# A post-norm decoder layer on one core: transposing softmax rows in halves, a residual sum kept in PSUM, and another order of VectorE and GpSimd work

## Chip, core and metric

The kernel runs on one core of a Trainium2 chip. The metric is the device time of one execution, in microseconds (us). The engines are PE (TensorE; PEld is its weight load), DVE (VectorE), ACT (ScalarE), POOL (GpSimd) and SP (SyncE, which issues most DMAs).

## What is computed

For 16 sequences of 128 rows of width 128, all in fp32:

```python
x = layernorm(x + attention(x))          # 16 heads of 64, softmax over 128 keys
x = layernorm(x + cross_attention(x, c)) # softmax over the 16 heads, inside each row
x = layernorm(x + feed_forward(x))       # light branch 64 wide, heavy branch 512 wide
```

The top-k of the reference takes 128 rows of 128, so the heavy branch is computed for every row.

## The kernel before, in words

**Steps.** One sequence of the batch is one unit of work, and three of them are in flight. In step s (0 to 15, then a tail written out by hand) the first attention of sequence s is begun (a), the first attention of s-1 is ended and its cross attention begun (b, c), and the cross attention of s-2 is ended (d). Some projections are made for four sequences at once, so the steps differ by their phase, s modulo 4: phase 0 has the larger part of the first attention's queries and keys, phase 1 has the keys of the cross attention, phase 2 has neither, and phase 3 begins the queries of the next group (`project_qk(g + 1, "A")`). Steps 3 to 14 run in a loop of four steps, three times; the others are written out. Every engine has its own list of instructions, in the order in which the program names them, and the engines wait for each other through counting semaphores (`wait_ge`).

**PE in a step** goes through this list, which L1242 to L1375 write out: transposes of the second eight heads of the step before (L1243); projections, if the phase has any; `values` (L1156); `weighted` (L1148, softmax times values); `scores(0)` (L1223, heads 0 to 7); `project_o` (L1168); `transpose_p2` (L1055); `scores(1)`; `values2` (L1162 to L1164); the transpose of x1 (L1308) and of the normalised x2 (L1083); `weighted_v2` (L1067); `project_q2` (L1136); transposes of the first eight heads (L1345); in phase 3 the first projections of the next group (L1028 to L1030); `project_o2` (L1076); `scores2` (L1178); in phases 3 and 0 further projections.

**The transposes of the softmax** (`transpose_p`, L1120; the instruction is L1127). A call makes four transposes of 128x128, one per head, into one PSUM bank; two calls make eight heads. ACT copies each bank to `pt` (L534).

**From scores to transposes.** DVE takes the row maxima of four heads at a time (`score_max`, L807), ACT makes the exponentials and their sums (L541, eight heads are q = 0 and 1, or 2 and 3), DVE inverts the sums of eight heads (`inverse_sums`, L813), POOL multiplies eight heads by them (L414) and PE transposes them.

**From project_o to x1.** DVE adds the residual to the bank of `project_o` (L769, `t1` lies in SBUF), takes the statistics (L771, L775), POOL makes the root (L383, L385), and DVE normalises (`x1_out`, L779). Between L775 and `x1_out` DVE does the two halves of `block_diagonal` (L718), of which PE's `weighted_v2` needs both. POOL waits for x1, adds a bias to it (L389), and then does L414.

**Behind project_q2** DVE takes out its two banks (`q2_out`, L785), and between them half of the cross attention's output (`regrouped`, L699; ACT does the other half at L499). `project_o2` waits for both halves and for the first `q2_out`, `scores2` for the second. In phase 3 the first projection of the next group waits for the first `q2_out`, the second for the second, the fourth for DVE's `regrouped`.

**First steps.** The weights of queries and keys come in five parts (`QK_PARTS`, L282) and are split into a high and a low fp32r part by ACT (L459) and DVE (L666). In step 1 DVE also scales and splits the weights of the feed forward (L915 to L920).

## Time and profile before

| | |
|---|---|
| runs of the kernel (us) | 406.04, 406.34, 407.11; median 406.34 |
| the profiled execution | 407.05 us, its span 405.2 us, granted clock 0.998 of full speed |
| busy in the span (us) | PE 394.5, PEld 343.2, DVE 286.9, ACT 240.5, POOL 146.7 |
| POOL's multiplications of the softmax, L414 | 32, 60.7 us |
| PE's transposes of the softmax, L1127 | 256, 34.6 us |

A busy PE is counted from the start of a product to its modelled end, and a product's neighbours overlap it. So the pace of PE is read from the start of one block of products to the start of the next, and not from the mean duration.

### The profile page before, as it was taken

To read this page: it belongs to the slowest core of one execution; us is meant where nothing else is said; L and a number is where in the kernel's file an instruction comes from. 1 tells how busy PE (TensorE), PEld (TensorE's weight loads), DVE (VectorE), ACT (ScalarE), POOL (GpSimd) and SP (SyncE) were. 2 spreads that over 40 slices of the span, in tenths; PEclk is the share of its full clock that TensorE was granted. 3 is DMA by queue.
4 is the path that set the end of the run, shared out by engine and by line. 5 is a ranking of instruction groups with operands and counts; after the bars stand their busy time and mean duration, and the time that the engine had idled before them with its cause. 6 is when DMAs were issued, how large, how long until landed. Compare 5 with 4: busy or idle time off the path is not lost.

```text
span 405.2 us, 15945 instructions
## 1 busy us (share of the span) xinstructions
PE 394.5 (97%) x6580; PEld 343.2 (85%) x6580; DVE 286.9 (71%) x662; ACT 240.5 (59%) x814; POOL 146.7 (36%) x223
## 2 busy tenths in 40 slices
PE   8999999999999999999999999999999999999995
PEld 7797788788888888788888888888988888898985
DVE  4685786865758687866849678676848778687645
ACT  5685664745666584745567475645558566555552
POOL 0541444331523354331413454422415454323314
PEclk9999999999999999999999999999999999999999
DMA  7900112210110213110110213100101111211001
GB/s 244 371 27 8 43 25 63 65 37 2 33 31 11 46 29 91 37 28 8 32 25 15 49 29 92 34 21 8 42 15 24 41 39 23 47 39 26 27 28 52
DMA packets 43758, 19.33 MB, mean 48 GB/s; under 512 B 36592, under 2 KB 41200, under 8 KB 43696
## 3 DMA queue, kind: packets, MB, share of 16 engines
q1 hardware_dynamic: 42880, 16.88, 16.1%
q0 software_dynamic: 528, 1.45, 1.0%
q8 instruction: 52, 0.85, 0.8%
q10 hardware_dynamic: 288, 0.07, 0.1%
q14 instruction: 10, 0.08, 0.1%
HBM read 8.95 MB, written 1.05 MB: 25 GB/s over the span
## 4 chain that ended last, share of the span: by engine, by line
PE 85%; DVE 6%; SPq 3%; issue 2%; ACT 2%; DMA 1%; POOL 0%; POOLq 0%; DVEq 0%
PE ps L1223 7%; PE ps L1168 7%; PE ps L1048 7%; PE ps L1076 7%; PE ps L1148 7%; PE ps L1127 6%; PE ps L1136 6%; PE ps L1028 5%; PE ps L1030 4%; PE ps L1029 4%; PE ps L1178 4%; PE ps L1067 3%; SPq L317 3%; PE ps L1104 3%; PE ps L1162 2%; PE ps L1156 2%
## 5 line engine op out<-in xcount | busy, mean ns | idle before, releaser
L541 ACT ACTIVATE p<-ps,neg_max 128x128 f32<-128x128 f32 x256 | 90.3, 385 | 40.8 <-DVE neg_max L807 40.8
L414 POOL TENSOR_TENSOR p<-p,row_inv 128x1024 f32<-128x1024 f32 x32 | 60.7, 1898 | 60.2 <-DVE row_inv L813 60.2
L534 ACT ACTIVATE pt<-ps 128x512 f32<-128x512 f32 x62 | 34.3, 624 | 48.6 <-PE ps L1127 48.5
L541 ACT ACTIVATION_READ_ACCUMULATOR p<-ps,neg_max 128x1 f32 x256 | 57.9, 226 | 0.0
L807 DVE TENSOR_REDUCE neg_max<-ps 128x4 f32<-128x512 f32 x64 | 41.6, 673 | 4.8 <-PE ps L1223 4.0
L753 DVE TENSOR_TENSOR ot<-ps,bv 128x512 f32<-128x512 f32 x32 | 22.0, 689 | 27.6 <-PE ps L1148 27.5
L1136 PE MATMUL ps<-x1t,wq 128*64 128x64 f32 x1024 | 33.8, 224 | 1.6 <-DVE v2s L763 0.9
L1127 PE MATMUL ps<-ident,p 128*128 128x128 f32 x256 | 34.6, 279 | 0.8 <-POOL p L414 0.8
L1223 PE MATMUL ps<-kt,qt 64*64 64x128 f32 x1024 | 35.2, 275 | 0.0
L1136 PEld LDWEIGHTS ps<-x1t,wq 128*64 128x64 f32 x1024 | 31.5, 138 | 3.0 <-issue 1.9
L1168 PE MATMUL ps<-wo,ot 128*128 128x128 f32 x256 | 32.7, 281 | 0.6 <-DVE ot L753 0.6
L1168 PEld LDWEIGHTS ps<-wo,ot 128*128 128x128 f32 x256 | 29.9, 191 | 3.3 <-issue 3.2
L1148 PEld LDWEIGHTS ps<-pt,v 128*64 128x64 f32 x512 | 27.6, 137 | 5.8 <-issue 5.8
L1223 PEld LDWEIGHTS ps<-kt,qt 64*64 64x64 f32 x1024 | 27.6, 132 | 5.5 <-issue 5.3
L1076 PE MATMUL ps<-wo,ot 128*128 128x128 f32 x256 | 31.9, 278 | 0.0
L1076 PEld LDWEIGHTS ps<-wo,ot 128*128 128x128 f32 x256 | 30.0, 192 | 1.8 <-issue 0.2
L1148 PE MATMUL ps<-pt,v 128*64 128x128 f32 x512 | 31.5, 276 | 0.0
L1127 PEld LDWEIGHTS ps<-ident,p 128*128 128x128 f32 x256 | 27.6, 141 | 3.6 <-POOL p L414 0.9
L1048 PE MATMUL ps<-cg,wk 128*64 128x128 f32 x512 | 29.7, 274 | 0.0
L394 POOL TENSOR_TENSOR rn<-ssm,minus_half 128x1 f32<-128x1 f32 x16 | 8.8, 551 | 55.9 <-DVE ssm L744 55.9
L1048 PEld LDWEIGHTS ps<-cg,wk 128*64 128x64 f32 x512 | 27.8, 137 | 1.2 <-issue 1.0
L1028 PE MATMUL ps<-xg_hi,wqk_hi 128*128 128x512 f32 x63 | 26.2, 416 | 2.2 <-DVE qt L785 1.4
(152 smaller groups left out, 835.5 us busy)
## 6 DMA issues: line engine op xcount, KB each, us to landing
v<-v2s SPq DMA_DIRECT2D x256, 32.0 KB
xg<-x_t SPq DMA_DIRECT2D x4, 256.0 KB, 2.9
cg<-ctx_t SPq DMA_DIRECT2D x4, 256.0 KB, 3.4
wo<-w_o SPq DMA_DIRECT2D x2, 512.0 KB, 9.5
xres<-x_nat SPq DMA_DIRECT2D x15, 64.0 KB, 1.8
pt<-w_qk SPq DMA_DIRECT2D x3, 256.0 KB, 4.3
out<-x2b SPq DMA_DIRECT2D x3, 256.0 KB, 2.3
x2b<-w_v SPq DMA_DIRECT2D x1, 512.0 KB, 7.3
```

What stands on the lines that cost most here:

```text
L414: nc.gpsimd.tensor_tensor(ph, ph, row_inv[:, 8 * half:8 * half + 8].unsqueeze(2).to_broadcast([T, 8, T]), ALU.mult).then_inc(p_ready, 1)
L534: nc.scalar.activation(pt[:, u * BANK:(u + 1) * BANK], bank(T_BANK[u]), ACT.Copy).then_inc(pt_ready, 1)
L541: last = nc.scalar.activation(p[:, hd * T:(hd + 1) * T], bank(S_BANK[q])[:, pos * T:(pos + 1) * T], ACT.Exp, bias=neg_max[:, hd:hd + 1], a ...
L807: nc.vector.reduce_max(neg_max[:, first:first + 7:2], bank(S_BANK[q]).rearrange("p (h k) -> p h k", h=4), AX.X, negate=True).then_inc(max_ ...
L1028: nc.tensor.matmul(out_cols, w_hi_cols, m_hi, start=True, stop=False)
L1048: last = nc.tensor.matmul(bank(BLOCK_BANKS[blk][r])[64 * ih:64 * ih + 64, i * 128:(i + 1) * 128], wk2[:, hd * DH:(hd + 1) * DH], own, star ...
L1076: last = nc.tensor.matmul(bank(O2, D), ot2[:, k * 128:(k + 1) * 128], wo2[:, k * D:(k + 1) * D], start=k == 0, stop=k == K - 1)
L1127: last = nc.tensor.transpose(bank(T_BANK[u])[:, i * T:(i + 1) * T], p[:, hd * T:(hd + 1) * T], ident[:])
L1136: last = nc.tensor.matmul(bank(Q2[u])[64 * ih:64 * ih + 64, i * HALF:(i + 1) * HALF], wq2[:, hd * DH:(hd + 1) * DH], x1t[:, ih * HALF:(ih ...
L1148: last = nc.tensor.matmul(bank(PV_BANK[u])[64 * (i % 2):64 * (i % 2) + 64, (i // 2) * T:(i // 2 + 1) * T], v[b_par][:, hd * DH:(hd + 1) * ...
L1168: last = nc.tensor.matmul(bank(O, D), ot[:, c * T:(c + 1) * T], wo[:, c * D:(c + 1) * D], start=c == 0, stop=c == NC - 1)
L1223: mm = nc.tensor.matmul(bank(S_BANK[2 * half + i % 2])[qh * HALF:(qh + 1) * HALF, (i // 2) * T:(i // 2 + 1) * T], qt[rows, first:first + H ...
```

## The change

- `transpose_p` takes eight heads in a call. Each head is transposed in two halves of 64 rows: the half e reads rows 64e to 64e+63 of `p` and the matching corner of the identity and writes 64 columns. The two halves of a head go to two different banks, so that a bank ends with half the queries of eight heads and no longer with four whole heads; ACT's copies put the pieces where they belong (`pt_part`, runs of 64 elements). Both banks of eight heads are released together at the end.
- `t1` is now the bank of `project_o` itself: the sum is written back to PSUM, and the statistics and `x1_out` read it there. `weighted_v2`, which writes that bank, waits for x1 and no longer for the sum.
- POOL multiplies the first eight heads right behind the root and adds the bias to x1 after that.
- DVE inverts the first eight sums between the two halves of `block_diagonal`, ahead of `x1_out`. `regrouped` goes ahead of both `q2_out` in phases 0 to 2 and behind both in phase 3.
- Step 1 on DVE: `score_max(2)` ahead of `x1_out`, the second inversion between the two `q2_out`. The high part of the feed forward's weights is made by ACT in step 2, the low part by DVE at the end of step 2.
- The first part of the query weights has 256 columns and not 128, and the third projection's two products with the high weights go ahead of the wait for the low ones.

```diff
...
@@ -195,6 +194,14 @@
+        def pt_part(u):
+            half, e = u // 2, u % 2
+            return (pt[:, half * 8 * T:(half + 1) * 8 * T].rearrange("p (h e q) -> p e h q", h=8, e=2)[:, e],
+                    bank(T_BANK[u]).rearrange("p (h q) -> p h q", h=8))
+        t1 = bank(O, D)
         def ot2_half(k2):
@@ -279,7 +286,7 @@
-        QK_PARTS = [slice(0, 128), slice(128, BANK)] + [slice(u * BANK, (u + 1) * BANK) for u in range(1, 4)]
+        QK_PARTS = [slice(0, 256), slice(256, BANK)] + [slice(u * BANK, (u + 1) * BANK) for u in range(1, 4)]
         HALVES = [slice(0, BANK), slice(BANK, 2 * BANK)]
@@ -383,6 +390,8 @@
                 nc.gpsimd.tensor_tensor(rs1[:], ve1[:], minus_half[:, 0:1], ALU.pow).then_inc(rs1_ready, 1)
+            def x1_biased(s, b_par):
                 if isinstance(s, int) and s == 1:
@@ -393,6 +402,13 @@
                 nc.gpsimd.tensor_tensor(x2b[:, bass.ds((s - 2) * D, D)], x2[:], bdl_row[:], ALU.add).then_inc(x2b_ready, 1)
+            def over_sum(s, half):
+                pool.wait_ge(inv_ready, 2 * s + half + 1)
+                ph = p[:, half * 8 * T:(half + 1) * 8 * T].rearrange("q (h k) -> q h k", h=8)
+                nc.gpsimd.tensor_tensor(ph, ph, row_inv[:, 8 * half:8 * half + 8].unsqueeze(2).to_broadcast([T, 8, T]),
+                                        ALU.mult).then_inc(p_ready, 1)
@@ -406,13 +422,12 @@
                     rstd1(s, b_par)
-                for half in range(2):
-                    if a:
-                        pool.wait_ge(inv_ready, 2 * s + half + 1)
-                        ph = p[:, half * 8 * T:(half + 1) * 8 * T].rearrange("q (h k) -> q h k", h=8)
-                        nc.gpsimd.tensor_tensor(ph, ph, row_inv[:, 8 * half:8 * half + 8].unsqueeze(2).to_broadcast([T, 8, T]),
-                                                ALU.mult).then_inc(p_ready, 1)
+                if a:
+                    over_sum(s, 0)
+                if bc:
+                    x1_biased(s, b_par)
+                if a:
+                    over_sum(s, 1)
                 if d:
...
@@ -531,7 +547,8 @@
                     act.wait_ge(mm_t, 4 * s + u + 1 if u < 2 else 4 * s - 4 + u + 1)
-                    nc.scalar.activation(pt[:, u * BANK:(u + 1) * BANK], bank(T_BANK[u]), ACT.Copy).then_inc(pt_ready, 1)
+                    dst, src = pt_part(u)
+                    nc.scalar.activation(dst, src, ACT.Copy).then_inc(pt_ready, 1)
@@ -607,6 +624,9 @@
                     exponentials(3)
+                if static and s == 2:
+                    act.wait_ge(wup_scaled, 2)
+                    nc.scalar.activation(wup_hi[:], wup, ACT.Copy).then_inc(wup_split, 1)
                 if static and s == 0:
...
@@ -766,9 +787,9 @@
                 dve.wait_ge(xres_ready, s)
-                nc.vector.tensor_tensor(t1[:], bank(O, D), xres[b_par][:], ALU.add).then_inc(sum1_ready, 1)
+                nc.vector.tensor_tensor(t1, bank(O, D), xres[b_par][:], ALU.add).then_inc(sum1_ready, 1)
                 dve.wait_ge(sum1_ready, s)
-                nc.vector.bn_stats(st1[:], t1[:]).then_inc(stats1_ready, 1)
+                nc.vector.bn_stats(st1[:], t1).then_inc(stats1_ready, 1)
@@ -776,7 +797,7 @@
                 dve.wait_ge(rs1_ready, s)
-                nc.vector.tensor_scalar(x1[:], t1[:], mv1[:, 0:1], rs1[:, 0:1], ALU.subtract, ALU.mult).then_inc(x1_ready, 1)
+                nc.vector.tensor_scalar(x1[:], t1, mv1[:, 0:1], rs1[:, 0:1], ALU.subtract, ALU.mult).then_inc(x1_ready, 1)
@@ -852,7 +873,12 @@
                     block_diagonal(s, 0)
+                if a and bc:
+                    inverse_sums(0)
+                if d:
                     block_diagonal(s, 1)
+                if static and s == 1:
+                    score_max(2)
                 if bc:
@@ -871,8 +897,7 @@
                     return
-                if a:
-                    inverse_sums(0)
+                if a and not (static and s == 1):
                     score_max(2)
@@ -889,16 +914,19 @@
                         dve.wait_ge(in_own_j, 16)
+                    if d and phase < 3:
+                        regrouped(s)
                     q2_out(s, 0)
-                if d:
-                    regrouped(s)
-                if bc:
+                    if static and s == 1:
+                        inverse_sums(1)
                     q2_out(s, 1)
+                    if d and phase == 3:
+                        regrouped(s)
                 if phase == 0 and a and bc:
                     qk_out(g + 1, "A")
-                if a:
+                if a and not (static and s == 1):
                     inverse_sums(1)
@@ -914,8 +942,7 @@
                     nc.vector.tensor_scalar(wup[:, FH:FP], wup[:, FH:FP], gam[:, 0:1], D ** 0.5, ALU.mult, ALU.mult).then_inc(wup_scaled, 1)
-                    dve.wait_ge(wup_scaled, 2)
-                    nc.vector.tensor_copy(wup_hi[:], wup).then_inc(wup_split, 1)
+                if static and s == 2:
                     dve.wait_ge(wup_split, 1)
@@ -1117,15 +1144,18 @@
-            def transpose_p(n, u):
-                if u % 2 == 0:
-                    pe.wait_ge(p_ready, 2 * n + u // 2 + 1)
-                for i in range(4):
-                    hd = 4 * u + i
-                    last = nc.tensor.transpose(bank(T_BANK[u])[:, i * T:(i + 1) * T], p[:, hd * T:(hd + 1) * T], ident[:])
-                last.then_inc(mm_t, 1)
+            def transpose_p(n, half):
+                pe.wait_ge(p_ready, 2 * n + half + 1)
+                for i in range(8):
+                    hd = 8 * half + i
+                    for e in range(2):
+                        rows = slice(HALF * e, HALF * e + HALF)
+                        mm = nc.tensor.transpose(bank(T_BANK[2 * half + e])[:, i * HALF:(i + 1) * HALF],
+                                                 p[rows, hd * T:(hd + 1) * T], ident[rows, rows])
+                        if i == 7:
+                            mm.then_inc(mm_t, 1)
@@ -1234,14 +1264,18 @@
                     nc.tensor.matmul(bank(FIRST_BANKS[0]), wqk_hi[:, 0:128], xg_lo[:], start=False, stop=True).then_inc(mm_qk, 1)
+                    project_qk(0, "A", lambda r: None, FIRST_BANKS, units=(1,))
+                    pe.wait_ge(w_hi, 2)
+                    nc.tensor.matmul(bank(FIRST_BANKS[2]), wqk_hi[:, 256:384], xg_hi[:], start=True, stop=False)
+                    nc.tensor.matmul(bank(FIRST_BANKS[2]), wqk_hi[:, 256:384], xg_lo[:], start=False, stop=False)
                     pe.wait_ge(w_lo, WQK_SPLIT[0])
-                    project_qk(0, "A", lambda r: None, FIRST_BANKS, units=(1, 2, 3))
+                    nc.tensor.matmul(bank(FIRST_BANKS[2]), wqk_lo[:, 256:384], xg_hi[:], start=False, stop=True).then_inc(mm_qk, 1)
+                    project_qk(0, "A", lambda r: None, FIRST_BANKS, units=(3,))
                     pe.wait_ge(w_lo, WQK_SPLIT[1])
                 if bc:
-                    transpose_p(s - 1, 2)
-                    transpose_p(s - 1, 3)
+                    transpose_p(s - 1, 1)
                 if phase == 0 and a and bc:
@@ -1315,7 +1349,7 @@
                     if bc:
-                        pe.wait_ge(sum1_ready, s)
+                        pe.wait_ge(x1_ready, s)
                     weighted_v2(s, 0)
...
```

## Rows read from the trace of the kernel before

**Rows 1.** The profile page, busy time of the engines in the span.
```profile
PE 394.5 (97%) x6580; PEld 343.2 (85%) x6580; DVE 286.9 (71%) x662; ACT 240.5 (59%) x814; POOL 146.7 (36%) x223
```

**Rows 2.** Waits of PE: who waited for whom, us in total, times, longest.
```profile
PE ps L1028 <- DVE qt L785: 1.4, 3, 0.5
...
PE ps L1168 <- DVE ot L753: 0.6, 1, 0.6
```

**Rows 3.** Timeline of PE, step 10 (phase 2): start, us, instruction, count, idle before.
```profile
235.85 0.27 PE L1308 MATMUL ps<-perm,x 128*128 128x128 f32 x1
...
237.25 2.09 PE L1136 MATMUL ps<-x1t,wq 128*64 128x64 f32 x64
239.27 1.09 PE L1127 MATMUL ps<-ident,p 128*128 128x128 f32 x8
240.30 2.02 PE L1076 MATMUL ps<-wo,ot 128*128 128x128 f32 x16
242.26 1.16 PE L1178 MATMUL ps<-kb,qt 64*64 64x64 f32 x64
243.35 0.33 PE L1127 MATMUL ps<-ident,p 128*128 128x128 f32 x1
```

**Rows 4.** Timeline of PE, step 15, the transposes and what follows.
```profile
347.40 1.09 PE L1127 MATMUL ps<-ident,p 128*128 128x128 f32 x8
348.33 0.50 PE L1076 MATMUL ps<-wo,ot 128*128 128x128 f32 x3
```

**Rows 5.** The profile page, weight loads of two lines: busy, mean ns of one.
```profile
L1168 PEld LDWEIGHTS ps<-wo,ot 128*128 128x128 f32 x256 | 29.9, 191 | 3.3 <-issue 3.2
...
L1127 PEld LDWEIGHTS ps<-ident,p 128*128 128x128 f32 x256 | 27.6, 141 | 3.6 <-POOL p L414 0.9
```

**Rows 6.** Timeline of PE, step 11 (phase 3) into step 12 (phase 0).
```profile
258.25 0.39 PE L1030 MATMUL ps<-xg_hi,wqk_lo 128*128 128x512 f32 x1
259.12 0.50 PE L1028 MATMUL ps<-xg_hi,wqk_hi 128*128 128x512 f32 x1 [0.48 <-DVE qt L785]
...
264.28 0.50 PE L1028 MATMUL ps<-xg_hi,wqk_hi 128*128 128x512 f32 x1
264.62 0.39 PE L1029 MATMUL ps<-xg_lo,wqk_hi 128*128 128x512 f32 x1
264.85 0.40 PE L1030 MATMUL ps<-xg_hi,wqk_lo 128*128 128x512 f32 x1
...
266.57 0.48 PE L1028 MATMUL ps<-xg_hi,wqk_hi 128*128 128x512 f32 x1
```

**Rows 7.** Timeline of DVE, step 10, and the end of `pick_own` in step 11.
```profile
234.04 1.26 DVE L718 TENSOR_TENSOR pt<-ps,mask 128x512 f32<-128x512 f32 x2
235.22 0.34 DVE L779 TENSOR_SCALAR x<-t,mv,rs 128x128 f32<-128x128 f32 x1
235.47 0.20 DVE L813 RECIPROCAL row_inv<-row_sum 128x8 f32<-128x8 f32 x1
...
238.46 0.69 DVE L785 TENSOR_TENSOR qt<-ps,bq 128x512 f32<-128x512 f32 x1 [0.44 <-PE ps L1136]
239.06 1.09 DVE L699 COPY ot<-ps 128x512 f32<-128x512 f32 x1
...
264.94 1.52 DVE L797 SCALAR_TENSOR_TENSOR s<-ps,own_j,s 128x256 f32<-128x256 f32 x3
```

**Rows 8.** Timeline of ACT, step 10: last exponential of heads 0 to 7; two copies.
```profile
234.62 0.24 ACT L541 ACTIVATION_READ_ACCUMULATOR p<-ps,neg_max 128x1 f32 x1
...
244.04 1.09 ACT L534 ACTIVATE pt<-ps 128x512 f32<-128x512 f32 x2 [2.77 <-PE ps L1127]
```

**Rows 9.** Timeline of POOL, step 10, the second eight heads.
```profile
240.86 1.90 POOL L414 TENSOR_TENSOR p<-p,row_inv 128x1024 f32<-128x1024 f32 x1 [2.91 <-DVE row_inv L813]
```

**Rows 10.** Timeline of PE at the start, the second unit of queries.
```profile
6.92 0.50 PE L1028 MATMUL ps<-xg_hi,wqk_hi 128*128 128x512 f32 x1 [0.76 <-DVE wqk_lo L666]
```

**Rows 11.** Timeline of DVE in step 1, the feed forward's weights.
```profile
49.35 0.82 DVE L920 TENSOR_TENSOR wup_lo<-x2b,wup_hi 128x640 fp32r<-128x640 f32 x1
```

## What was predicted

> **What bounds the kernel now.** I read the page first: PE is busy in 394.5 of 405.2 us [rows 1]. As the ends of products are modelled, that alone proves little, so I then asked what PE waits for. The list is short: 1.4 us in three places for DVE's `q2_out` and 0.6 us once for `attention_out` [rows 2], besides some waits of the first and last steps. Then the timeline of PE: between two blocks there is no idle time in a step of phase 2 [rows 3]. So the time is the sum of PE's blocks, and a block made shorter is worth its whole difference, until something that PE needs behind it comes too late. The other engines are idle a third of the time or more, but they have due times, and the question of each edit is whether it moves a due time past PE.
>
> The sums are made against the profiled execution, 407.05 us; it lies 0.71 us above the median of 406.34, so I take the difference off the median.
>
> **Transposes in halves.** Eight heads take PE 1.03 us from the start of their block to the next (239.27 to 240.30) [rows 3]. In step 15 the same block takes 0.93 us (347.40 to 348.33) [rows 4]: the 0.10 more, and 0.08 more in the block behind it (240.30 to 242.26 is 1.96 for sixteen products), is a wait of `project_o2` for DVE's `regrouped`, which ends at 239.06 + 1.09 = 240.15, next to PE's 240.30 [rows 7]. So the transposes themselves take 0.93 / 8 = 0.116 us per head. No transpose of 64 rows is in the trace. The nearest block is L1136: 64 products that move 64 columns each, two at a time on two halves of the array, 2.02 us, which is 0.063 us per pair [rows 3]. A head in two halves would be such a pair: 8 x (0.116 - 0.063) = 0.42 us less per block, 32 blocks. The other end is that the two halves of a head don't overlap, or that the weight load sets the pace: then the block keeps its 0.93 us. I take the pair's pace, because L1178 runs halves of rows and of columns at once, sixteen groups of four in 1.09 us (242.26 to 243.35 is the next block, the transposes of step 11), 0.068 us a group [rows 3].
>
> On loads: a load of 128 columns for a transpose has a mean of 141 ns, that of `project_o`'s weights of the same shape 191 ns [rows 5], so the transposes' load is the quicker one and need not be the bound of a pair at 63 ns, if the loads of the two halves overlap.
>
> The halves make the array tiled, and PE pays for the change back to the whole array. Where L1028 follows the tiled L1178, its first product stands 0.34 us ahead of the second (264.28 to 264.62), an ordinary one 0.23 (264.62 to 264.85) [rows 6]; with what the block before it loses at its end I take 0.17 us per change (0.1 to 0.25). Block by block, with the phase of the step in which it stands:
> - First eight heads, phases 0 to 2: 0.42 - 0.17 for the change to `project_o2` + 0.17 for the wait for `regrouped`, which goes (below): 0.42.
> - First eight heads, phase 3: behind them comes the first projection of the next group, which waits for `q2_out`, and that is barely earlier: 0.15 (0 to 0.25).
> - Second eight heads, phase 1: tiled blocks on both sides: 0.42. Phases 2 and 3: 0.42 - 0.17 = 0.25. Phase 0: PE goes on at 266.57 as soon as `pick_own` has ended, at 264.94 + 1.52 = 266.46 [rows 6, 7]; it will wait there for the same moment: 0.
>
> ACT's two copies now begin together, at the end of a block that ends earlier; two take 1.09 us [rows 8], and they are released no later than now. That their runs of 64 elements cost more is possible: DVE takes 1.09 us for the scattered 512 of `regrouped` and 0.69 us for `q2_out` [rows 7], so up to 1.6 times. I take no more, since a run of 64 is nearer to the plain copy; the upper end goes into the range.
>
> **`regrouped`.** In phases 0 to 2 it moves ahead of the first `q2_out`. DVE was idle for 0.44 us before that one, so `regrouped` can begin at 238.02 and not at 239.06 [rows 7]; with what x1 is late (below) it ends about 0.8 us earlier, which removes the 0.17 us above. The first `q2_out` then begins about 0.93 us (the pace of `regrouped`) behind it, some 0.7 us later than now, and ends about 0.1 us ahead of PE's earlier `project_o2`; the second ends no later than now. In phase 3 the second projection stood 259.12 - 258.25 = 0.87 behind the last product of the first, against 0.23: 0.64 us lost to the second `q2_out`, which stands behind `regrouped` [rows 6]; with `regrouped` behind both, this goes, and `regrouped` is due only at the fourth projection, 1.4 us later: +0.64 in each of three steps [rows 2].
>
> **The inversion ahead of x1.** This one costs. In step 10 the first half of `block_diagonal` ends at about 234.04 + 0.62 = 234.66. The inversion that now comes next needs the sums of the eighth exponential, and that is there at 234.62 + 0.24 = 234.86 [rows 7, 8]. DVE is in order, so the second half of `block_diagonal` and `x1_out` stand behind this wait: inversion from 234.89, the second half from 235.00 (now 234.62), `x1_out` from 235.60 (now 235.22), 0.38 us later [rows 7]. `x1_out` ends now at 235.56, PE's transpose of x1 begins at 235.85 [rows 3, 7]; of these 0.29 us I take half as slack, since PE must still take the release and load. So PE waits 0.38 - 0.15 = about 0.22 us in each step with a cross attention end (0.1 to 0.38). Nothing in the new PSUM sum changes that: the sum and the statistics come before the wait, which has 0.2 us of cover. Behind it only `x1_out` itself reads PSUM; for 128 columns no such row exists, so I leave it at 0.34 us, with 0.05 either way. The wait of `weighted_v2` for x1 costs nothing, since PE has waited for x1 one block earlier (L1307).
>
> **POOL.** The first eight heads are multiplied ahead of the bias and so earlier; nobody waits for that, as PE's first block shows no wait for POOL [rows 3]. The bias comes about one multiplication (1.90 us [rows 9]) later, and is due a step later. The second eight heads: POOL ends at 240.86 + 1.90 = 242.76, PE begins them at 243.35 [rows 3, 9]; 0.59 of cover, of which the shorter first block takes 0.42; 0.17 is left.
>
> **First steps.** The second unit of queries began after 0.76 us of idle time on PE [rows 10]. That goes, but the third weight part and a larger first DMA set the next due times; 0.4 us (0 to 0.7). In step 1 x1 comes about 0.5 us later, behind `score_max(2)`, but PE waits for the second eight heads anyway: +0.1. The split of the feed forward's weights, of which the low part alone takes 0.82 us on DVE [rows 11], stands ahead of `attention_out` of step 2, for which PE lost 0.6 us [rows 2]: +0.6, less 0.1 in step 3 for the low part.
>
> **The sum.** A turn of four steps: second eight heads 0 + 0.42 + 0.25 + 0.25 = 0.92; first eight heads 3 x 0.42 + 0.15 = 1.41; phase 3's projection 0.64; x1 -4 x 0.22 = -0.88; together 2.1 us. Three turns: 6.3. Steps 0 to 2: 0.4 + 0.1 + 0.6 - 0.1, with 0.25 + 0.42 for step 2's blocks and -0.15 for its x1 (the transposes of step 0 save nothing, as PE waits there for ACT's copies): 1.5. Step 15: 0.25 + 0.25 - 0.22 = 0.3. Tail: 0.25. Together 8.4 us: profiled 398.6, median **397.9 us**.
>
> **Rivals.** (1) Slower: the weight load of 128 columns sets the pace of the pair. Two loads of half the rows take no less than one of all rows, and a pair takes the 0.11 us of a head today. For it: PE has never loaded 128 columns more quickly than one in 0.11 us on average (27.6 us for 256) [rows 5]; against it the 141 ns and L1178's four loads in 0.068 us. Then the blocks save nothing, the changes of the array cost 0.17, and a turn gives second heads -0.45, first heads -0.1, projection 0.64, x1 -0.88: -0.8; three turns -2.4, first steps +0.8, step 15 and tail -0.7: 2.3 us slower, 408.6 us. It decides from a pair of about 0.10 us on. (The Trainium skill, "TensorE: Matmul & The Clock Gate", section "LDWEIGHTS (loading the stationary operand)", says that a load takes time by its columns and not by its rows, with 107 ns for 128 columns as an estimate from its formula. By that rule this rival would be the outcome; the 141 ns of the transposes' load, beside 191 for the same shape, does not agree with one price per column.) (2) The next waits eat the first blocks: `project_o2` meets the first `q2_out`, now behind `regrouped`, and the second heads meet POOL; then some 0.3 us of each step is lost, 13 steps: 401.8 us. For it: covers of 0.1 and 0.17 us only. (3) x1 is not late, because the exponentials end before DVE is there: +0.22 x 13 = 2.9 us: 395.0 us. Against it: 0.2 us in the trace. (4) ACT's copies at 1.6 times: 0.65 us more per pair of copies, against some 0.25 of cover, in seven steps without projections: +2.8 us, 400.7 us.
>
> **Numbers.** Forecast 0.57, (1) 0.10, (2) 0.17, (3) 0.11, (4) 0.05. The forecast's own ends, from the changes at 0.1 or 0.25, the x1 wait at 0.1 or 0.38 and the start, are 396 to 400. The range takes in (2), (4) and most of (3): 394.5 to 402.5. A measurement of this kernel tells about 0.3%, 1.2 us, from no change. Faster 0.87, the same 0.04, slower 0.09.
>
> **What would show it.** Right: the transposes' block at 0.5 to 0.6 us from start to start; PE's transpose of x1 with 0.2 us of idle time behind DVE's x1, and DVE idle ahead of the early inversion for `exp_ready`; no wait of the second projection in phase 3; `project_o` of step 2 without a wait. Wrong: the block still at 0.9 us, or new waits of PE ahead of `project_o2`, `weighted` or the second eight heads.

## The result, and the profile after

The changed kernel takes 403.57 us (median of four, 403.26 to 405.40) beside 406.48 for the kernel before: ratio 0.9936, 95% interval 0.9908 to 0.9964. Ten more runs of it in the first experiment had a median of 404.86 (ratio 0.995, 0.9933 to 0.9968). So it is faster, by 1.7 to 2.9 us where 8.4 were forecast, and the time lies above the range. The profiled execution took 405.40 us with a span of 403.59.

From the page of the changed kernel, the row that answers to [rows 1], and the queue that carries instructions (packets, MB, share of the DMA engines):

```profile
PE 389.4 (96%) x6836; PEld 335.5 (83%) x6836; DVE 288.7 (72%) x661; ACT 240.4 (60%) x815; POOL 147.0 (36%) x223
...
q8 instruction: 54, 0.88, 0.9%
```

PE is busy 5.1 us less than in [rows 1], and the span is only 1.7 us shorter: something new stands between the blocks. What PE waited for in the changed kernel (us in total, times, longest), the answer to [rows 2]:

```profile
PE ps L1103 <- DVE ot L720: 1.6, 1, 1.6
PE ps L1166 <- issue: 1.5, 3, 0.6
...
PE ps L1208 <- DVE qt L806: 0.8, 1, 0.8
...
PE ps L1155 <- issue: 0.6, 1, 0.6
PE ps L1342 <- DVE x L800: 0.5, 2, 0.3
```

The waits of [rows 2] are gone or shorter. In their place stand waits in `project_q2` (L1166) and at the transposes (L1155) put down to "issue", that is, to nothing that the profile shows.

Step 10 of the changed kernel on PE, to be laid beside [rows 3]:

```profile
233.28 0.40 PE L1194 MATMUL ps<-wv_lo,cg_hi 128*128 128x512 f32 x1
233.78 0.30 PE L1342 MATMUL ps<-perm,x 128*128 128x128 f32 x1
...
234.14 1.16 PE L1094 MATMUL ps<-pt,v 64*64 64x64 f32 x64
235.23 2.08 PE L1166 MATMUL ps<-x1t,wq 128*64 128x64 f32 x64
237.89 0.71 PE L1155 MATMUL ps<-ident,p 64*128 64x64 f32 x16 [0.57 <-issue]
238.53 2.05 PE L1103 MATMUL ps<-wo,ot 128*128 128x128 f32 x16
240.51 0.87 PE L1208 MATMUL ps<-kb,qt 64*64 64x64 f32 x44
```

The transposes' block is 0.64 us from start to start (237.89 to 238.53) instead of 1.03. Ahead of x1's transpose PE stands 0.26 us longer than before: 233.28 to 233.78 is 0.50, and in the kernel before it was 235.62 to 235.85 [rows 3]:

```profile
235.62 0.39 PE L1164 MATMUL ps<-wv_lo,cg_hi 128*128 128x512 f32 x1
```

And before the transposes there is a hole, a pause of 0.57 us with nothing to release it.

The same step on DVE, beside [rows 7]:

```profile
231.72 0.66 DVE L739 TENSOR_TENSOR pt<-ps,mask 128x512 f32<-128x512 f32 x1
232.56 0.20 DVE L834 RECIPROCAL row_inv<-row_sum 128x8 f32<-128x8 f32 x1 [0.18 <-ACT p L558]
232.68 0.64 DVE L739 TENSOR_TENSOR pt<-ps,mask 128x512 f32<-128x512 f32 x1
233.24 0.40 DVE L800 TENSOR_SCALAR x<-ps,mv,rs 128x128 f32<-128x128 f32 x1
```

This is the forecast's picture: the inversion waits for the exponential, the second half of `block_diagonal` and `x1_out` stand behind it.

### The profile page after: what moved, and what is told of

Same layout as the page of the kernel before. It is cut to its first block, busy times and chain, and to the rows that moved or that the text cites. A ratio compares the mean times of both kernels' runs of the same rounds, so it can differ in the third digit from the quotient of the medians.

```text
span 403.6 us, 16457 instructions
## 1 busy us (share of the span) xinstructions
PE 389.4 (96%) x6836; PEld 335.5 (83%) x6836; DVE 288.7 (72%) x661; ACT 240.4 (60%) x815; POOL 147.0 (36%) x223
## 4 chain that ended last, share of the span: by engine, by line
PE 88%; DVE 3%; ACT 3%; issue 2%; DMA 2%; POOL 1%; SPq 1%; POOLq 0%; DVEq 0%
PE ps L1253 8%; PE ps L1103 8%; PE ps L1198 7%; PE ps L1075 7%; PE ps L1166 7%; PE ps L1178 7%; PE ps L1055 5%; PE ps L1155 5%; PE ps L1057 4%; PE ps L1056 4%; PE ps L1094 4%; PE ps L1208 4%; PE ps L1131 3%; PE ps L1192 2%; PE ps L1186 2%
## 5 line engine op out<-in xcount | busy, mean ns | idle before, releaser
L1166 PE MATMUL ps<-x1t,wq 128*64 128x64 f32 x1024 | 34.3, 224 | 1.9 <-issue 1.5
L1166 PEld LDWEIGHTS ps<-x1t,wq 128*64 128x64 f32 x1024 | 31.7, 138 | 3.5 <-issue 2.5
L1056 PE MATMUL ps<-xg_lo,wqk_hi 128*128 128x512 f32 x62 | 24.5, 395 | 0.0
L1057 PE MATMUL ps<-xg_hi,wqk_lo 128*128 128x512 f32 x62 | 24.5, 395 | 0.0
```

The costliest lines, as they stand in the source:

```text
L1056: nc.tensor.matmul(out_cols, w_hi_cols, m_lo, start=False, stop=False)
L1057: return nc.tensor.matmul(out_cols, w_lo_cols, m_hi, start=False, stop=True)
L1166: last = nc.tensor.matmul(bank(Q2[u])[64 * ih:64 * ih + 64, i * HALF:(i + 1) * HALF], wq2[:, hd * DH:(hd + 1) * DH], x1t[:, ih * HALF:(ih ...
```

## The experiments

Four questions were open. F: are the holes late transfers of TensorE's instructions? X: what does the late x1 cost? H: what are the halves worth by themselves? And do the answers add up to a quicker kernel? Besides whole times I use one stretch of each profile, from the weighted values (`weighted_v2`) of step 3 to those of step 15. These are twelve steps free of the start and the tail; they take 269.04 us in the kernel before, and 267.53 in the changed kernel's first profile.

### F: where instruction pieces begin

I numbered TensorE's loads, products and waits in order of start. Every hole of the changed kernel's loop lies at a number that is 193 above a multiple of 256, and the 54 transfers of instructions are 16 KB each, one for every 256 of the 13854 numbers. I call the place where a new piece of 256 begins a border. One such hole, in step 5, on PE and on its loads:

```profile
131.45 0.39 PE L1166 MATMUL ps<-x1t,wq 128*64 128x64 f32 x5 [0.57 <-issue]
...
131.45 0.25 PEld L1166 LDWEIGHTS ps<-x1t,wq 128*64 128x64 f32 x5 [0.71 <-issue]
```

(The Trainium skill, "Advanced Engine Details and Errata", section "ISA Cache", gives a cache line of 16 KB or 256 instructions, and only two lines. The size agrees with the trace; the number of lines no run here tests.)

**e1_again**: no edit.

> The changed kernel once more, nothing altered, as the measure for the three beside it. Theory F (late instruction transfers): in the profile of the changed kernel TensorE stands still 0.60 to 0.79 us at its instructions number 4289, 8385, 10945 and 11713 in order of start, all of them 193 above a multiple of 256, each time 1.3 to 1.5 us after a 16 KB transfer of the instruction queue has ended; if the cause is where the 256-instruction pieces begin, the same four places, and no others between the numbers 2000 and 12000, stand still again, by 0.5 to 0.9 us each, and the time is 403.5 (403 to 405.5). Rival R (the pauses come from traffic that differs from one execution to the next): the pauses lie at other numbers.

Measured: 404.86 us (403.27 to 406.19, ten runs), stretch 266.20. From the traces, holes of over 0.3 us at such borders in steps 3 to 15: number, us between the starts on both sides, and us from the end of the transfer to the first instruction behind the border:

```
changed kernel     4289 0.79 1.46   8385 0.69 1.48   10945 0.60 1.29   11713 0.79 1.28
the same again     4289 0.33 1.38   7617 0.42 1.27   11713 0.61 1.19   12481 0.35 1.47
x1 first (e3)      3265 1.27 1.44   4289 0.55 1.26    5057 0.38 1.52   10945 0.63 1.34
halves only (e4)   3265 0.66 1.32   4289 0.63 1.52    7617 0.87 1.27    8385 0.41 1.45   10945 0.54 1.32
kernel before     11969 0.91 1.32
```

Two of the four expected places stood still again, and two others did; so the expectation of the same four was wrong, but no hole lies off a border. Which border is late in an execution changes (a transfer takes 0.9 to 1.5 us); where one can be late does not. In these five traces a transfer starts 1.8 us before to 3.4 us after PE enters the piece ahead; PE can go on 1.2 to 1.5 us after its end. The holes all end pieces that hold `weighted_v2`, `project_q2` and the transposes, where 256 instructions pass in 3.0 to 5.1 us with the hole taken out; other pieces as short had an earlier transfer and no hole. The halves add 32 instructions per step just there.

**e2_shift96**: idle products move the borders.

```diff
+                if static and s == 1:
+                    for _ in range(24):
+                        nc.tensor.matmul(bank(2)[:, 0:2], warm[:], warm[:, 0:2], start=True, stop=True)
                 if a and bc:
```

> The changed kernel with 24 tiny products (2 columns, in the profile 48 loads and 48 products) in step 1, where TensorE waits 0.7 us for ScalarE's copies; they compute nothing that is used. They shift every later instruction by 96 against the 256-instruction pieces. In the profile of the changed kernel 9 pieces run through in under 4.7 us; with the borders moved by 96 only 1 would. Theory F: the pauses at 4289, 8385, 10945, 11713 and the long one of step 15 go, 3 to 4 us, against some 0.5 us that the tiny products cost beyond the wait: 2 to 3.5 us below the changed kernel of the same call, about 400.5. Rival R: no gain, 0 to 0.7 us slower.

Measured: 409.73 us (ratio to before 1.0078, 1.0057 to 1.0099), stretch 264.39 with no hole at a border. Whole, it is slower, against the expectation: the tiny products took 6.5 us at a place where the changed kernel stands 0.7, and the granted clock, 1.00 ahead of them, fell. Two windows (length, PE, PEld, DVE, ACT, POOL busy, clock, DMA share, GB/s):

```profile
30.00:36.60 6.60, 6.60 (x56) 6.53 (x53) 1.60 (x3) 1.81 (x4) 0.00 (x0) 0.83 0.01 2
36.60:44.00 7.40, 7.40 (x78) 6.02 (x79) 2.09 (x4) 1.19 (x2) 0.00 (x0) 0.69 0.00 0
```

Each tiny product still loads 128 columns of weights, 48 x 0.135 us; I had priced them by their two columns.

**e5_pad112**: waits instead of products; they use no array.

```diff
+            padding = [224]
+
+            def pad():
+                for _ in range(min(6, padding[0])):
+                    pe.wait_ge(warm_set, 1)
+                    padding[0] -= 1
             def product3(out_cols, w_hi_cols, w_lo_cols, m_hi, m_lo):
+                pad()
                 nc.tensor.matmul(out_cols, w_hi_cols, m_hi, start=True, stop=False)
...
```

Two calls of `wait_ge` became one instruction: 224 calls, 112 instructions more in the trace.

> The changed kernel with 112 more instructions on TensorE's queue in step 0 that only wait for a semaphore long since set, up to three ahead of each product of 512 columns (about 50 ns each, beside products that start every 235 ns), so that the borders of the 256-instruction pieces move by 112 and no product is added that could cost the clock. With the borders there, 1 or 2 pieces run through in under 4.7 us in the changed kernel's profile, where 9 do now. Theory F: no pause at a border from step 3 to step 14, where the two profiles of the changed kernel had 2.7 and 1.6 us of them; 1.5 to 3 us below the changed kernel, 401 to 402.5. Rival R: the time of the changed kernel, 403.5 to 405.

Measured: 404.26 us (0.992, 0.9889 to 0.995), stretch 264.43, no hole. The whole time missed the expected 401 to 402.5: the 3.1 or 1.8 us gained in the stretch went into step 0, from the first product of the input to the first scores 15.1 us instead of 11.7 to 12.2. Waits in a row start 0.106 us apart in the trace, so three fill more than the 0.235 us from product to product, which became 0.34.

**e9_pad111_spread**: one wait per product, and three groups of 23 (the edit against e5's, cut).

```diff
-                for _ in range(min(6, padding[0])):
+            def pad(n=2):
+                for _ in range(n):
...
+                    pad(46)
                     pe.wait_ge(w_lo, WQK_SPLIT[2])
...
+                    if static and s == 1:
+                        pad(46)
                     pe.wait_ge(pt_ready, 4 * s - 4 + 2)
...
+                    if static and s == 1:
+                        pad(46)
                     pe.wait_ge(x1t_ready, s)
```

> The changed kernel with 111 waits for a semaphore long since set, as in e5, but spread: one ahead of each of 42 products of 512 columns in step 0 and 23 at each of three places in steps 0 and 1 where TensorE stands 0.7 to 1.0 us anyway. In e5 they took the pauses out of the loop (281.9 us from the weighted values of step 2 to those of step 15, against 283.8 and 285.2 in two profiles of the changed kernel), but step 0 became 2.3 to 2.9 us longer. Theory F: the loop stays at 282, step 0 costs under 0.7 us: 401 to 402.5. Rival R (the gain of the loop in e5 is chance, or comes back elsewhere): 403.5 to 405.

Measured: 405.50 us (0.9974, 0.9961 to 0.9987), above the expected 401 to 402.5; stretch 264.27, no hole, and step 0 at 11.8 us, so a single wait per product is free. The groups in step 1 are not (first group, second group, and a window with the granted clock in its third last column):

```profile
28.82 1.21 PE L1169 MATMUL ps<-ident,p 64*128 64x64 f32 x32
31.68 0.47 PE L1200 MATMUL ps<-wv_hi,xg_lo 128*128 128x512 f32 x1 [1.66 <-ACT pt L551]
...
43.94 1.34 PE L1180 MATMUL ps<-x1t,wq 128*64 128x64 f32 x20 [2.48 <-issue]
...
44.00:60.00 16.00, 15.81 (x305) 13.50 (x309) 10.90 (x25) 7.33 (x29) 6.35 (x8) 0.90 0.18 39
```

The first wait was 0.7 us in the changed kernel, the second 0.4. I had assumed that a group is worked off while TensorE has products ahead of it and stands anyway. But 23 waits that start 0.106 us apart take 2.4 us, and of the first group only seven or eight lie under the transposes ahead. The second pause cost more than itself: behind it the granted clock was 0.50 from 44 to 46 us, the level of 1.2 GHz, and `project_q2` took 3.52 us and not 2.14. Two waits behind it, of 0.8 and 0.3 us, went in return, so from `project_q2` to the `weighted_v2` of step 2 it takes 15.8 us instead of 15.4.

**e12_after_shift**: only the places that were free, and key products of step 0 (the edit against e9's, cut; the two groups of step 1 are gone).

```diff
+            k2_padding = [46]
...
+                            if k2_padding[0]:
+                                k2_padding[0] -= 1
+                                pad()
                             last = nc.tensor.matmul(bank(BLOCK_BANKS[blk][r])[64 * ih:64 * ih + 64, i * 128:(i + 1) * 128],
```

> The changed kernel with 111 waits more in step 0 alone, where e9 showed them to cost nothing: one ahead of each of 42 products of 512 columns and 23 in one place where TensorE stands 1 us (steps 0 to the first scores took 11.8 us in e9, as without them), and, new, one ahead of each of 46 of the second layer's key products, which start every 206 ns. The two groups of step 1 that cost 1.0 and 2.1 us are gone. Three kernels with shifted borders (e2, e5, e9) took 264.4, 264.4 and 264.3 us from the weighted values of step 3 to those of step 15, against 267.5 and 266.2 for the changed kernel. Theory F: 264.4 again, and step 0 within 0.5 us, so 401 to 402.5 in all. Rival R: 403.5 to 405.

Measured: 402.19 us (401.72 to 402.54; 0.9885, 0.9865 to 0.9904), stretch 264.30, no hole. Step 10, without one:

```profile
234.43 2.08 PE L1184 MATMUL ps<-x1t,wq 128*64 128x64 f32 x64
236.45 0.71 PE L1173 MATMUL ps<-ident,p 64*128 64x64 f32 x16
237.09 2.05 PE L1121 MATMUL ps<-wo,ot 128*128 128x128 f32 x16
239.07 1.16 PE L1226 MATMUL ps<-kb,qt 64*64 64x64 f32 x64
240.16 0.71 PE L1173 MATMUL ps<-ident,p 64*128 64x64 f32 x16
```

Four kernels with moved borders took 264.3 to 264.4 us in the stretch, the changed kernel 267.53 and 266.20; laid beside e12 block by block, each of its two profiles loses this time at five borders, but for 0.1 us. In none of the fifteen traces does PE pass a border sooner than 1.2 us after the end of its transfer, and in the kernels with moved borders the shortest such time in the stretch is 2.8 us. F stands: the holes cost 3.2 and 1.9 us, and the kernel before had none over 0.3 us in this stretch (its one hole lies behind, in step 15).

### X: the late x1

**e3_x1_first**: DVE's old order ahead of x1.

```diff
                     block_diagonal(s, 0)
-                if a and bc:
-                    inverse_sums(0)
-                if d:
                     block_diagonal(s, 1)
-                if static and s == 1:
-                    score_max(2)
                 if bc:
                     x1_out(s)
+                if a and bc:
+                    inverse_sums(0)
+                if static and s == 1:
+                    score_max(2)
```

> The changed kernel with VectorE's order ahead of the normalised sum put back: the normalised sum x1 is written before the inverse of the first eight heads' sums, behind both block-diagonal copies. The order of TensorE is untouched, so the borders of the instruction pieces stay. Theory X: TensorE's wait at the transpose of x1, 0.3 us longer per step in the changed kernel, goes in 12 to 14 steps, 3 to 4 us: about 400. Rival Y (the inverse, now later, makes GpSimd's division and so the transposes of the first eight heads late, or the time is lost again at the pauses F): within 1 us of the changed kernel.

Measured: 400.53 us (399.32 to 401.95; 0.9842, 0.9816 to 0.9868). DVE and PE in its step 10:

```profile
230.23 1.26 DVE L739 TENSOR_TENSOR pt<-ps,mask 128x512 f32<-128x512 f32 x2
231.40 0.40 DVE L800 TENSOR_SCALAR x<-ps,mv,rs 128x128 f32<-128x128 f32 x1
231.72 0.19 DVE L834 RECIPROCAL row_inv<-row_sum 128x8 f32<-128x8 f32 x1
...
231.80 0.40 PE L1193 MATMUL ps<-wv_lo,cg_hi 128*128 128x512 f32 x1
232.04 0.27 PE L1341 MATMUL ps<-perm,x 128*128 128x128 f32 x1
...
232.35 1.16 PE L1093 MATMUL ps<-pt,v 64*64 64x64 f32 x64
```

No wait for the exponential any more, and x1's transpose follows at the ordinary 0.24 us. It came 0.26 us sooner in steps 4 to 14 and 0.07 in step 3. X stands, Y falls.

**e11_whole_x1**: the same edit in e7 (below).

> e7 (whole transposes, the rest of the change) with x1 ahead of the inverse. In e3 that order gave 0.26 us in each of 14 steps. Theory X (its price doesn't depend on the transposes): 3.0 to 3.9 us below e7, 403.5 to 404.4, so that the other orders of VectorE are worth 2.5 us against the kernel before. Rival Y: within 1 us of e7.

Measured: 403.17 us (ratio to before 0.9912, 0.9891 to 0.9932) against e7's 407.40, a little below the expected range; stretch 265.60 against 268.79: 3.19 us, 0.27 per step. With the halves the same edit, together with one in step 15 that lies outside the stretch, gives 264.43 to 261.03, 3.40 us (e5 to e6). So the price hardly depends on the transposes.

### H: the halves alone, and all but the halves

**e4_halves_only**: the kernel before with the changed `transpose_p` and copies.

```diff
-                for i in range(4):
-                    hd = 4 * u + i
-                    last = nc.tensor.transpose(bank(T_BANK[u])[:, i * T:(i + 1) * T], p[:, hd * T:(hd + 1) * T], ident[:])
+                for i in range(8):
+                    hd = 8 * half + i
+                    for e in range(2):
+                        rows = slice(HALF * e, HALF * e + HALF)
+                        mm = nc.tensor.transpose(bank(T_BANK[2 * half + e])[:, i * HALF:(i + 1) * HALF],
+                                                 p[rows, hd * T:(hd + 1) * T], ident[rows, rows])
```

> The kernel before with the transposes in row halves alone (and ScalarE's copies that put the halves in order); the sum goes through SBUF, VectorE's and GpSimd's order and the first products are as before. By my steps: first eight heads 0.25 per step where 0.42 held the wait for the regrouped copy, which stays here; second eight 0.42 in phase 1 and 0.25 in phases 2 and 3; over 13 steps some 4.5 us, so 402. Theory F adds that its dense stretch holds 32 instructions more per step, and pauses of 0.6 to 0.9 us appear in some steps where a border falls there: 402 to 405.5, and the blocks themselves 0.64 us from start to start of the next group instead of 1.03. Rival W (weight loads set the pace): blocks still 1.0 us, time 406 or more.

Measured: 405.10 us (0.9971, 0.9957 to 0.9986), stretch 268.02 with five holes, 3.1 us together. The blocks are 0.65 us from start to start, so W falls. But where no hole stands ahead of it (steps 6, 8 and 12) `project_o2` now waits longer for `regrouped` and starts as late as before; in step 6:

```profile
150.21 2.02 PE L1084 MATMUL ps<-wo,ot 128*128 128x128 f32 x16 [0.26 <-DVE ot L707]
152.16 1.16 PE L1189 MATMUL ps<-kb,qt 64*64 64x64 f32 x64
153.25 0.71 PE L1136 MATMUL ps<-ident,p 64*128 64x64 f32 x16
153.90 0.50 PE L1167 MATMUL ps<-wv_hi,xg_lo 128*128 128x512 f32 x1
```

Alone the halves are worth 1.5 us: of the first eight heads little is left without the new order, and most of the rest goes into the holes.

**e7_whole**: the changed kernel with the old `transpose_p` and copies.

```diff
                     transpose_p(s, 0)
+                    transpose_p(s, 1)
...
```

> The changed kernel with the transposes of whole heads as before (and ScalarE's plain copies); the sum in PSUM, the order of VectorE and GpSimd and the first products stay changed. By the steps that the traces bear out, the halves are worth 0.25 us per step in the first eight heads and 0.4, 0.2 and 0.2 in the second eight of phases 1 to 3, some 5 us in all, against about 1.5 us more of pauses at the borders of instruction pieces: theory H says 407 to 408.5, at or above the kernel before, since x1 remains 0.3 us late. Rival W (the halves give little, most of the gain is VectorE's order): 404 to 405.5.

Measured: 407.40 us (0.9999, 0.9973 to 1.0025), stretch 268.79. H stands: without the halves the change gives nothing, as its new orders gain what the late x1 costs. Its step 10 shows the blocks without a wait:

```profile
239.21 1.09 PE L1152 MATMUL ps<-ident,p 128*128 128x128 f32 x8
240.13 1.95 PE L1101 MATMUL ps<-wo,ot 128*128 128x128 f32 x16
242.01 1.16 PE L1203 MATMUL ps<-kb,qt 64*64 64x64 f32 x64
```

### A kernel from the answers

**e6_x1_pad_f**: e3 with e5's waits, and in step 15 `regrouped` first.

```diff
-                if static and s == B - 1:
-                    f_low(0)
...
-                    if d and phase < 3:
+                    if d and (phase < 3 or static):
                         regrouped(s)
...
+                if static and s == B - 1:
+                    f_low(0)
```

> Three edits to the changed kernel: x1 ahead of the inverse (as in e3), the 112 waits of e5, and in step 15 the low half of the last group's normalised rows behind the regrouped copy, which itself goes ahead of the two query blocks there as it does in phases 0 to 2. Theory F and X add up: e3 took 400.5; its profile holds 2.6 us of pauses at borders that go, and the wait for the regrouped copy in step 15, 1.2 to 1.8 us in three profiles, shrinks by about 1.2 us: 396.7 (395.5 to 398). Rival R: only the step 15 term, 399.3. If the saved time is eaten by the next wait, 400.5.

Measured: 400.24 us (0.9833, 0.9794 to 0.9873), above the expected 395.5 to 398. The stretch is 261.03, 3.5 below e3's 264.57, but e5's waits cost 3.3 us in step 0 here as well (15.1 for 11.8); from step 15 to 16 18.53 us instead of 19.06, so the wait for `regrouped` gave 0.5 and not 1.2.

**e8_best_sbuf**: e6 with the sum in SBUF.

```diff
-        t1 = bank(O, D)
+        t1 = sb("t1", [T, D])
...
-                        pe.wait_ge(x1_ready, s)
+                        pe.wait_ge(sum1_ready, s)
                     weighted_v2(s, 0)
```

> e6 with the sum of attention output and residual in SBUF again, as in the kernel before, and the wait of the weighted values back on the sum. VectorE's three steps on it took 0.29, 0.30 and 0.34 us from SBUF and 0.30, 0.30 and 0.40 from PSUM, and the step that writes x1 ends the way to TensorE's transpose. Theory S: PSUM costs 0.05 to 0.08 us per step where x1 is awaited, so 0 to 1.0 us below e6. Rival P (the sum in PSUM gains by itself): 0.5 us or more above e6.

Measured: 399.83 us (0.9842, 0.9795 to 0.9889), stretch 260.78. This can't be told from e6 by time; P, a gain by PSUM of 0.5 us or more, isn't there.

**e10_best**: e8 with e9's waits.

> e8 (x1 ahead of the inverse, the regrouped copy first in step 15, the sum in SBUF) with the spread waits of e9 in place of those of e5. From e8's 399.8 the 2.3 to 2.9 us that its waits cost in step 0 come off but for 0.7: 397.7 (396.5 to 398.5). If the spread waits cost as much, 399.8.

Measured: 400.13 us (0.9842, 0.982 to 0.9865), above the expected range again; stretch 260.75: the groups in step 1 cost 3.1 us here: from the first scores to the weighted values of step 2 it takes 41.0 us, e13 (below) 37.9.

**e13_best**: e8's edits with e12's waits.

> e10 (x1 ahead of the inverse, the regrouped copy first in step 15, the sum in SBUF, shifted borders) with the waits placed as in e12. e10 lost 3.0 us in step 1 to its waits (from the weighted values of step 3 to those of step 15 it took 260.75 us): 400.1 less 2.5 to 3.0, 397.3 (396.8 to 398). If the waits cost as much in their new place, 400.

Measured: 397.28 us (median of six, 396.79 to 400.86), ratio 0.9787, 0.9753 to 0.982; stretch 260.77. This beats both kernels, by 9.3 us and by some 7. The longest waits of PE in it after the first product:

```profile
PE ps L1182 <- DVE v2s L783: 0.9, 1, 0.9
PE ps L1202 <- ACT pt L550: 0.7, 1, 0.7
PE ps L1449 <- DVE x L799: 0.7, 1, 0.7
```

These are in step 1 and behind step 15; the others are 0.3 us or less. From 74 to 334 us, the stretch of the loop, the list of waits is empty.

## Why the forecast was too low

The direction was right, the size wrong. Us of span, minus is faster; measured in the two profiles of the changed kernel against that of before:

| part | forecast | first profile | again |
|---|---|---|---|
| start, to the first scores | -0.4 | +0.44 | -0.33 |
| from there to `weighted_v2` of step 3 | -1.1 | -0.45 | -0.56 |
| steps 3 to 15, holes taken out | -6.3 | -4.74 | -4.74 |
| holes at instruction borders | 0 | +3.23 | +1.90 |
| step 15 | -0.3 | +0.36 | +0.36 |
| tail | -0.25 | -0.49 | -0.32 |
| sum | -8.4 | -1.65 | -3.69 |

"Holes taken out" is e12's 264.30 against 269.04; the holes are the rest.

**The step that failed: the sum of PE's blocks.** "A block made shorter is worth its whole difference, until something that PE needs behind it comes too late": I looked for this among what other engines deliver, and three of the four rivals name such waits. What came too late were PE's own instructions. The halves double the number of transposes, and I priced the 512 additional instructions (256 loads, 256 products) by the array alone. The trace of before held a hint: in step 15 its `project_q2` stands still for 0.9 us in its middle, at one of these borders (11969), and I passed over it. The holes are 1.9 to 3.2 of the 4.7 to 6.7 us that are missing.

**Halves: mis-sized.** In the stretch they were to give 5.5 us (2.25 and 0.45 for the first eight heads in phases 0 to 2 and 3, 2.76 for the second); e7 to e12 is 4.5, with a short hole of e7 in it. The second eight give 0.38 in phase 1 (forecast 0.42) and 0.19 to 0.20 in phases 2 and 3 (0.25). The pair came as forecast: inside a block the pairs start 0.062 us apart. What was too long is the whole head. I took 0.93 / 8 = 0.116 us, and that has the block's two ends in it; in the trace of before the transposes inside a block start 0.109 us apart. 8 x (0.109 - 0.062) is 0.38 us, what phase 1 gives with tiled blocks on both sides. Where a block on the whole array follows, 0.18 to 0.19 of it is lost, about the 0.17 that I took: a block in e12 is 0.64 us and the one behind it 1.98 (237.09 to 239.07), together 2.62 against e7's 2.80. Rival (1) was wrong, as the loads of the transposes in the changed kernel show (ns of one, least, median, most):

```profile
L1155 PEld LDWEIGHTS ps<-ident,p x512: 134/139/142, 29.1 to 350.7; 64*128 64x128 f32 x171
```

A load of a half lasts as long as that of a whole did, 139 ns to 141 [rows 5], but the two of a pair start together, every 0.062 us, so several run at once and the pace isn't theirs. (The section "LDWEIGHTS (loading the stationary operand)" of the Trainium skill's "TensorE: Matmul & The Clock Gate" says that a load takes time by its columns and not by its rows. That the rows don't count agrees with the trace; that the columns do doesn't, since loads of 64 columns last 138 ns there as well (L1166). The pace that the rival made of it doesn't follow.)

**`regrouped` and phase 3: right.** 3.45 us in the stretch were forecast (nine times 0.17, three times 0.64). e7 has these orders and the late x1 and stands 0.25 below before; its x1 costs 3.19 (e11), so the orders give 3.4. Block by block, e7 takes 0.17 us less in each of nine steps (2.81 for the two blocks that took 2.98) and 0.75 less in each of three, 3.8 together; part of the difference is a hole of 0.3 us in e11.

**x1: right in kind, too cheap.** The row with the inversion's wait of 0.18 us is as forecast, but 0.22 us per step became 0.31. x1's transpose comes 0.26 us later, and from there to `weighted_v2` it takes 0.36 us (233.78 to 234.14) where x1 is awaited and 0.31 (232.04 to 232.35) where it isn't. Over the stretch that makes 3.2 us (e7 to e11) to 3.5 (e12 to e13, which has the sum in SBUF too), where 2.6 were taken. The slack was the half of 0.29 us that I had taken: PE's transpose begins 0.14 us behind the end of `x1_out` (233.24 + 0.40 to 233.78). What the forecast lacks is `x1_out` from PSUM, 0.40 us where I had left it at 0.34 [rows 7], and the 0.05 us behind the wait. I charged this cost to the change and let it stand as given; that it was worth one third of the whole forecast, and that putting two lines back would have taken it away, was there to be said.

**Start: wrong.** The 0.76 us wait of [rows 10] goes, and the first scores come no sooner: 17.83 us before, 18.27 and 17.50 after, and 17.61 in e4, which has the old first products. The input's first product began at 5.22 us in the trace of before, at 6.03 and 5.81 in those of the changed kernel and at 6.02 in e4, where the old first products show no such wait either. So the wait seems to have been the other side of an early start; what sets that start (5.2 to 6.2 us over all traces) stays open, and whether any of the 0.4 us is there can't be told.

**Steps 1 to 3.** `project_o` of step 2 lost its 0.6 us wait as forecast; that of step 3 now waits 0.26 us behind the low part, for which 0.1 was taken. Missed was step 1, where the inversion of the second eight heads was put between the two query blocks; DVE waits for an exponential there, and PE for the query block:

```profile
43.97 0.20 DVE L834 RECIPROCAL row_inv<-row_sum 128x8 f32<-128x8 f32 x1 [0.78 <-ACT p L558]
44.09 0.64 DVE L806 TENSOR_TENSOR qt<-ps,bq 128x512 f32<-128x512 f32 x1
...
44.79 1.16 PE L1208 MATMUL ps<-kb,qt 64*64 64x64 f32 x64 [0.76 <-DVE qt L806]
```

It is the same kind of step as the early inversion, which I had followed in the loop and not here. By itself it is no loss: PE waited 0.90 and 0.76 us in step 1 before (for `values2_out` and for POOL), and waits 0.32, 0.41, 0.76 and 0.26 us there now. But the gain of 0.1 us that was forecast there did not come.

**Step 15.** It is phase 3 without a next projection, so `regrouped` stands behind both query blocks, and `f_low` ahead of them, with nothing on PE to cover it:

```profile
344.93 0.71 PE L1155 MATMUL ps<-ident,p 64*128 64x64 f32 x16
347.22 2.02 PE L1103 MATMUL ps<-wo,ot 128*128 128x128 f32 x16 [1.58 <-DVE ot L720]
```

I used the rule of phase 3 for the steps with a projection only, and forgot this one.

**The other rivals.** (2), at 401.8 us, came nearest, and that is luck: its waits, of `project_o2` for `q2_out` and of the second eight heads for POOL, are nowhere in the loop. (3) fell with the 0.18 us. (4) fell: copies in runs of 64 take 617 ns on average, the plain ones took 624, and nobody waits for them in the loop.

## What to carry to other kernels

Where an engine runs without gaps, count its instructions as well as its time: an edit that doubles short instructions in a dense stretch can lose there what it saves on the array, at places that depend on how many instructions stand ahead. When a profile shows waits for "issue" at odd places, number the instructions and look at what the numbers have in common; a few instructions more in a place that has time can move the borders. And before a step that waits is moved up on an engine that works in order, read what stands behind it in every step that has it, the first and the last ones too.

## What the runs showed of the hardware

- TensorE's instructions came in pieces of 256, one transfer of 16 KB each; PE went on 1.2 to 1.5 us after a transfer's end, and stood still 0.3 to 1.3 us where a piece of 3.0 to 5.1 us met a late one. Why some transfers start up to 3.4 us after the piece ahead is entered (up to 4.5 in the kernels with moved borders), and others before, stays open.
- A wait alone on TensorE's queue took 51 ns in the trace, and waits in a row started 0.106 us apart. One ahead of each product of 512 columns cost nothing, three made the 0.235 us from product to product 0.34, and groups of 23 made two pauses 1.0 and 2.1 us longer. Behind the longer pause, of 2.5 us, the granted clock was 0.50 for 44 to 46 us (e9).
- Products of two columns behind loads of 128 kept TensorE busy by the trace, 6.60 of 6.60 us, and the granted clock, 1.00 in the 10 us ahead, was 0.83 on average over those 6.6 us, 0.69 in the next 7.4 us and 1.00 in the 12 us behind them; its levels are 2.4 and 1.2 GHz (e2).
- Transposes of whole heads started 0.109 us apart, pairs of halves 0.062 us, and a tiled block with a whole-array block behind it lost 0.18 to 0.19 us of the difference (before, e7, e12).
